# Second sweep of a quantised feed-forward block: the fetches and the stores of one DMA queue in another order

## The reference

```python
x = act_qdq(x)                                   # scale = max|x| / 32767 over the whole tensor
up = act_qdq(x @ lpbq_dequant(w_up).T)           # 256 -> 768
gate = act_qdq(x @ lpbq_dequant(w_gate).T)
sig = fixed_qdq_u16(jax.nn.sigmoid(gate))        # round(sig * 65536) / 65536
gate = act_qdq(gate * sig)
o = act_qdq(gate * up)
return o @ lpbq_dequant(w_down).T
```

## Time and profile before

| | us |
|---|---|
| median of 3 runs | 2003.8 |
| the profiled execution | 2003.72 |
| its span in the trace | 2001.6 |
| TensorE, VectorE, ScalarE, GpSimd busy in the span | 1860.6, 1582.8, 1197.2, 418.0 |
| sweep 2, from its first product to the end of its last | 1573.5 to 1729.1 |
| stores of `gate_scratch`: count, size, median to landing | 28, 768 KB, 3.5 |
| fetches of `raw_scratch`: count, size, median to landing | 32, 768 KB, 5.9 |

### The profile page before, as it was taken

One profiled execution on the slowest core, in us unless ns is written; L12 is line 12 of the kernel. 1 busy time (PEld: TensorE's weight loads), 2 busy tenths in 40 slices (PEclk: granted clock), 3 DMA queues, 4 the chain that ended last, 5 costly groups with the idle time before them and its releaser, 6 DMA issues. The chain is left out here.

```text
span 2001.6 us, 70719 instructions
## 1 busy us (share of the span) xinstructions
PE 1860.6 (93%) x28023; PEld 1309.7 (65%) x28023; DVE 1582.8 (79%) x2870; ACT 1197.2 (60%) x2015; POOL 418.0 (21%) x516
## 2 busy tenths in 40 slices
PE   6999999999999968999999999999699988899798
PEld 4667666677666656888888888887344333344687
DVE  6777777777777765888888888887465799988897
ACT  4455444445444425777777777776355666688465
POOL 1112212211111121323232323232000222100121
PEclk9999999999999979999999999999699999899899
DMA  4111111111111011212121212120288788599574
GB/s 142 41 35 35 45 40 34 40 45 34 40 40 40 24 53 51 60 48 58 47 58 47 58 47 59 46 60 5 74 268 274 274 313 313 193 404 384 190 270 148
DMA packets 169444, 221.90 MB, mean 111 GB/s; under 512 B 80691, under 2 KB 142390, under 8 KB 169270
## 3 DMA queue, kind: packets, MB, share of 16 engines
q1 hardware_dynamic: 169270, 219.22, 33.0%
HBM read 116.40 MB, written 94.37 MB: 105 GB/s over the span
## 5 line engine op out<-in xcount | busy, mean ns | idle before, releaser
L1535 PE MATMUL ff_twin<-ff_xq,w_uh 128*128 (+1 forms) x1152 | 347.7, 384 | 38.4 <-DVE ff_top L1904 24.0
L1535 PEld LDWEIGHTS ff_twin<-ff_xq,w_uh 128*128 128x128 f16 x1152 | 111.1, 99 | 187.9 <-issue 43.9
L1535 PE MATMUL ff_twin<-ff_xq,w_ul 128*128 (+1 forms) x576 | 220.5, 383 | 0.0
L721 DVE TENSOR_TENSOR x<-rec_x,rec_until 128x512 f32<-128x512 f32 x256 | 159.0, 683 | 50.8 <-PE rec_x L401 50.8
L573 ACT ACTIVATE x<-rec_e,rec_hidden 128x512 f32<-128x512 f32 x256 | 158.0, 687 | 55.7 <-PE rec_e L418 55.7
L307 POOL TENSOR_TENSOR rec_o<-rec_tmp 128x512 f32<-128x512 f32 x32 | 68.2, 2131 | 561.9 <-DVE rec_tmp L771 561.9
L1266 DVE TENSOR_REDUCE mneg<-att_s 128x4 f32<-128x512 f32 x256 | 158.8, 682 | 26.8 <-PE att_s L1037 26.8
L541 ACT ACTIVATE rec_v<-rec_f 128x256 f32<-128x256 f32 x64 | 24.5, 383 | 213.7 <-DVE rec_z L730 213.7
L1183 ACT ACTIVATE att_e<-att_s 128x512 f32<-128x512 f32 x256 | 132.2, 612 | 21.3 <-PE att_s L1070 21.3
L748 DVE TENSOR_TENSOR rec_tmp<-rec_x,x 128x512 f32<-128x512 f32 x128 | 79.7, 683 | 82.4 <-POOL rec_o L309 70.0
L430 PE MATMUL rec_x<-x 32*32 32x64 f32 x8192 | 139.1, 218 | 4.2 <-issue 3.9
(11 more groups left out here) (245 smaller groups left out, 4436.1 us busy)
## 6 DMA issues: line engine op xcount, KB each, us to landing
raw_scratch<-ff_out SPq DMA_DIRECT2D x32, 768.0 KB, 3.5
ff_in<-raw_scratch SPq DMA_DIRECT2D x32, 768.0 KB, 5.9
gate_scratch<-ff_out SPq DMA_DIRECT2D x28, 768.0 KB, 3.5
ff_in<-gate_scratch SPq DMA_DIRECT2D x28, 768.0 KB, 9.1
product_scratch<-ff_out SPq DMA_DIRECT2D x28, 768.0 KB, 8.7
ff_out<-product_scratch SPq DMA_DIRECT2D x28, 768.0 KB, 5.9
turned_scratch<-rec_xT SPq DMA_DIRECT2D x32, 256.0 KB, 2.9
att_x<-in_x SPq DMA_DIRECT2D x32, 256.0 KB, 2.8
```

Source lines behind the costliest of these rows:

```text
L721: V.tensor_tensor(mt[:, b].rearrange("p (a j m) n -> p j a m n", a=KC, m=2)[:, j], X[j].rearrange("p (a m n) -> p a m n", a=KC, m=2), unti ...
L1535: m = T.matmul(bank_.rearrange("p (b n) -> p b n", b=BT), weights(wp, kc, a, c), tile[:, xp, :, kc], start=(i == 0), stop=(i == len(terms) ...
```

## The change

The SyncE program of sweep 2 is written in another order and without a loop. `refill` takes one half. For each step m the queue now holds: fetch of half 1 for step m + 1, store of product half 0 of step m, fetch of half 0 for step m + 2, store of product half 1 of step m. What each DMA waits for, the buffers, and the instructions of all other engines are as they were.

```diff
-                def refill(m, n):
-                    for s in range(2):
-                        sp.wait_ge(q["rounded"], m * FC + (s + 1) * HC)
-                        fetch_raw(n, s)
+                def refill(m, n, s):
+                    sp.wait_ge(q["rounded"], m * FC + (s + 1) * HC)
+                    fetch_raw(n, s)
...
-                with sp.Fori(0, NT // 2 - 2) as j:
-                    for u in range(2):
-                        refill(2 * j + u, 2 * j + u + 3)
-                        for s in range(2):
-                            store(g_d, 2 * j + u, 2 * j + u + 2, u, s)
-                for u in range(2):
-                    refill(NT - 4 + u, (NT - 1 + u) % NT)
-                    for s in range(2):
-                        store(g_d, NT - 4 + u, NT - 2 + u, u, s)
-                refill(NT - 2, 1)
+                refill(0, 3, 0)
+                for m in range(NT - 2):
+                    u = m % 2
+                    refill(m, (m + 3) % NT, 1)
+                    store(g_d, m, m + 2, u, 0)
+                    refill(m + 1, (m + 4) % NT, 0)
+                    store(g_d, m, m + 2, u, 1)
+                refill(NT - 2, 1, 1)
```

## The result

The changed kernel takes 2007.38 us (median of 17 runs), the kernel before 2001.85 us in 17 runs beside it: a ratio of 1.0032 with a 95% interval of 1.0022 to 1.0043, by the ratio 6.4 us slower (4.4 to 8.6); the two medians lie 5.5 us apart. The profiled execution of the changed kernel happened to be a quick one (2001.61 us, span 1999.5), for reasons that lie ahead of the feed-forward block: its sweep starts 6.0 us earlier (1567.51 against 1573.51), and VectorE's row of the attention that starts at 1265.93 before starts at 1259.77 after, 6.2 us earlier. So the sweep is read from its own windows.

The account below looks back on a forecast made before the run. VectorE, without a gap in sweep 2, was taken to bound the kernel; 14 holds of 0.54 us (7.56) less 0.19 us saved give +7.4 us on 2003.8: 2011.2 us, own range 2007.8 to 2013.1, 8-in-10 range 2003.0 to 2014.0.

Parts of the forecast that it names:

- VectorE bounds the step, and ScalarE's wait is no prize: Sweep 2: VectorE is busy 10.05 of 10.05 us a step; ScalarE's 42.8 us of waiting for fetches costs nothing.
- Where the fetch puts ScalarE: Sweep 2: ScalarE starts on half 0 at 8.16 us behind product(m, 0), some 3 us earlier than 11.2.
- The share moves under product 1, in 14 steps: Sweep 2: GpSimd's share (its `fixed_u` instruction) of half 0 runs at 12.1 to 13.6, with product(m+1, 1) due at 12.85.
- 0.54 us in each step: Sweep 2: VectorE's product 1 waits for GpSimd's share, overlap 0.68 less 0.14 us, in each of 14 steps.
- the 0.27 us that GpSimd takes behind its releaser: Sweep 2: delay from the end of product 0 to the start of GpSimd's share, taken as 0.27 us.
- Half 1's share at 5.7 in a step: Sweep 2: GpSimd's share of half 1 comes at 5.7 in a 10.6 us step, beside `largest`, and costs nothing.
- split over both halves: Sweep 2, a sign in the trace: ScalarE's wait for the fetch is no longer before half 0 alone.
- All behind the sweep unchanged: Behind sweep 2: the sweep gets 7 to 8 us longer and everything after it stays as it was.
- Rival 2: Sweep 2: share starts just ahead of product 1, at most 1.33 us lost a step, 18.6 us, 2022; chance 0.08.
- Rival 4: Sweep 2: share and product pass each other without a hold, 2003.6 us; chance 0.27 together with Rival 1.
- Rival 1: Sweep 2: late fetch puts the share behind product 1, GpSimd waits, 2003.6 us; chance 0.27 together with Rival 4.

Follow-up runs that it names:

- Two experiments that take only this meeting away: Changed kernel with GpSimd's half 0 share waiting for product(m - 1, 1): ratio 0.9993; changed kernel with VectorE's second `highest` ahead of product(m, 1): ratio 0.9995.
- the shifted share: Changed kernel with a tiny GpSimd operation ahead of half 0's share, so that it starts some tenths of a us later: ratio 1.0050.
- the run in which it was made late: Changed kernel with GpSimd's share of half 0 waiting for product(m - 1, 1) instead of product(m - 1, 0): ratio 0.9993.
- the relieved kernel of the old order: Kernel before, with `largest` in sweep 2 taken over 64 of 1536 columns: 1983.60 us, one run.

## Why the prediction was right, point by point

- *VectorE bounds the step, and ScalarE's wait is no prize*: right. ScalarE waits as long for its fetches as before, 44.3 us after and 42.8 before.
- *Where the fetch puts ScalarE*: 8.16 predicted, 8.14 measured in the step shown, 7.9 to 8.2 in all of them.
- *The share moves under product 1, in 14 steps*: right from the first, product(1, 1), on. Two experiments that take only this meeting away, one on each engine, take the loss away.
- *0.54 us in each step*: 0.47. The step that was mis-sized is the 0.27 us that GpSimd takes behind its releaser. Behind VectorE it is 0.19. The overlap is then 0.60 and the wait, less 0.13, 0.47: 14 x 0.47 - 0.19 = 6.4 where 7.4 stood. The 0.27 was read behind ScalarE, and the kernel before gave no steady step in which a share waits for VectorE.
- *Half 1's share at 5.7 in a step*: it comes at 5.20, released by product 1; it lies beside reductions as foretold, and costs nothing. The step towards it was wrong: half 1's fetch does not put ScalarE at 12.4, two transfers behind half 0, but ScalarE goes on to it almost at once, at 11.83 (1610.85). So the wait for the fetch is not split over both halves, as the last paragraph of the prediction has it: 2.4 of the 44.3 us are before half 1. The stores land 4.4 us behind their issue instead of 3.5 (medians), later as foretold, and no wait for them shows.
- *All behind the sweep unchanged*: wrong, by 1.4 to 1.5 us. The last share ends 3.85 instead of 0.58 us ahead of the sweep's last maximum, and what GpSimd goes through before its reduction, for which VectorE had waited, begins that much earlier. The wait was in the profile before (1.42 us behind 1724.86); I had read the sweep only to its last maximum.
- The sum by the traces is then 6.34 - 1.50 = +4.84 us; forecast +7.4; timed +6.4 (4.4 to 8.6). The forecast of 2011.2 was against a kernel before of 2003.8 us; this kernel's median over all its runs is 2001.85. So the 2007.38 lie just under the forecast's own range of 2007.8 to 2013.1 by its numbers, and 6.4 and 4.84 both lie inside it as differences (4.0 to 9.3). The range was wide enough to hold the sum with 0.03 in place of 0.27 as well: that the mechanism and its sizes are right is shown by the trace and the experiments, and the time alone would not have told it.
- *Rival 2* (a share that starts later costs more) did not come about, but its mechanism is real: the shifted share shows it, 0.86 us in a step. *Rival 4* (the hold is not what three cases say) is out. *Rival 1* was not what happened; that a share behind the product costs nothing is shown by the run in which it was made late.

## What to carry to other kernels

When the engine that bounds a loop never idles, making its suppliers earlier gains nothing by itself; ask instead which of its instructions the earlier work will now lie beside. A GpSimd instruction like this share, which reads SBUF, makes a VectorE product wait that comes due while it is under way; the same instruction beside a reduction is free, so place it there by a wait or by VectorE's order, or, for a part of the gain, cut it in pieces. Read on behind the loop: an engine that ends its part earlier may start something long that the next stage waits for.

## What the runs showed of the hardware

- Of a product and a share, the one that comes second waits for the overlap less 0.13 or 0.14 us, whoever it is (overlap and wait): 0.32 and 0.19, 0.60 and 0.47, 0.99 and 0.86, 1.22 and 1.08 with VectorE second, 1.10 and 0.96, 0.87 and 0.73 with GpSimd second. The longest is in the relieved kernel of the old order, where a product starts at 1574.28, 0.07 behind a share: 1.40 of overlap, and it takes 3.00 us. With the share in three pieces the hold is 0.20 to 0.29 us: it ends with the instruction in flight and not with the run of instructions.
- A one-input multiplication from int16 to float32 takes 0.94 us for 1536 elements, a two-input one 1.74, a maximum 1.74; the first two are held, the maximum is not.
- A GpSimd memset of 1.38 us under a product holds nothing (overlap 1.23, product 1.75), and is not held.
- From the end of GpSimd's last tensor operation of the sweep to the reduction over partitions 5.6 to 6.2 us pass, in every one of the eleven traces.
